# Taking the sixteen Q/K column tiles in the order of their numbers, in a fused attention and quantized-FFN layer on eight cores

## What is computed

```python
xn = layernorm(x)
q, k, v = split(xn @ w_in.T)                  # 16 heads of 64
# windows of 512 tokens; a query sees its own window up to itself
# and the 512 keys before itself (its own and the preceding window)
p = softmax(q @ k.T / 8 + slope[h] * (qi - kj))
attn = (p @ v) @ w_out.T
x_scale = max|xn| per token / 127;  x_q = round(xn / x_scale)
ffn = (x_q @ weight_q.T) * x_scale * weight_scale + bias
out = x + attn + ffn
```

## Time and profile before

| | us |
|---|---|
| median of 2 runs (3992.86 to 4000.87) | 3996.86 |
| the profiled execution, its own time | 3986.59 |
| its span, core 3 (slowest) | 3984.7 |
| spans of the eight cores | 3949.1 to 3984.7 |
| TensorE busy (matmuls) | 2591.0, 65% |
| ScalarE busy | 1769.4, 44% |
| VectorE busy | 1371.6, 34% |
| mean granted TensorE clock | 0.705 of full |

### The profile page before, as it was taken

The page is one execution under the profiler, slowest core; times in us unless marked ns, Lnnn a source line. Parts: engine busy times, 40 slices in busy tenths (PEclk is TensorE's granted clock), DMA queues, the critical chain, the costliest instruction groups (busy, mean ns, idle before and its releaser), DMA issues.

```text
span 3984.7 us, 41683 instructions; the slowest of 8 cores (3949.1 to 3984.7 us)
## 1 busy us (share of the span) xinstructions
PE 2591.0 (65%) x10560; PEld 1031.4 (26%) x10560; DVE 1371.6 (34%) x3552; ACT 1769.4 (44%) x4033; POOL 4.4 (0%) x10
## 2 busy tenths in 40 slices
PE   0466675766766667576676657667576666766777
PEld 0122232222322223222232222223222222322322
DVE  0233342333423244242442423335233333423414
ACT  0252551825616173371733438164281525617355
POOL 0000000000000000000000000000000000000000
PEclk9867668576585857758667675866758677585776
DMA  8101102011020201102011010100101011020100
GB/s 156 62 28 52 36 15 74 5 50 39 13 77 6 85 4 38 50 6 85 4 36 54 32 58 6 61 27 26 63 5 56 34 47 41 11 79 4 42 26 26
DMA packets 79521, 161.00 MB, mean 40 GB/s; under 512 B 8770, under 2 KB 17218, under 8 KB 78914
## 3 DMA queue, kind: packets, MB, share of 16 engines
q1 hardware_dynamic: 76786, 147.85, 10.9%
q0 software_dynamic: 2512, 10.49, 1.6%
HBM read 119.51 MB, written 37.75 MB: 39 GB/s over the span
## 4 chain that ended last, share of the span: by engine, by line
PE 42%; ACT 15%; DMA 14%; DVE 12%; issue 9%; ACTq 5%; DVEq 3%; SPq 0%; POOLq 0%
PE ps L461 14%; ACT pe_buf L652 10%; DMA wqk<-w2bf 9%; PE ps L609 8%; PE ps L702 6%; PE ps L631 6%; PE ps L714 5%; ACTq L105 4%; DMA x_tm<-x 3%; DVEq L105 3%; PE ps L551 2%; ACT zln L533 2%; DVE stt L277 2%; DVE stt L279 1%; DVE pe_buf L665 1%
## 5 line engine op out<-in xcount | busy, mean ns | idle before, releaser
L652 ACT ACTIVATE pe_buf<-ps,ebias_sb 128x128 bf16<-128x128 f32 (+4 forms) x2560 | 912.8, 526 | 190.8 <-PE ps L631 182.6
L461 PE MATMUL ps<-xn_fm,wqk 128*128 128x512 bf16 x2048 | 599.8, 457 | 507.3 <-DMA wqk<-w2bf 506.5
L609 PE MATMUL ps<-pe_buf,v_st 128*65 128x128 bf16 (+3 forms) x2368 | 656.7, 399 | 346.1 <-DVE pe_buf L665 217.2
L665 DVE TENSOR_TENSOR pe_buf<-pe_buf,tripo_sb 128x128 bf16<-128x128 bf16 x1792 | 391.9, 223 | 1086.3 <-ACT pe_buf L652 1041.3
L631 PE MATMUL ps<-q_fm,k_st 64*128 64x512 bf16 (+3 forms) x1792 | 459.8, 434 | 231.5 <-ACT pe_buf L652 223.8
L461 PEld LDWEIGHTS ps<-xn_fm,wqk 128*128 128x128 bf16 x2048 | 220.9, 113 | 884.8 <-issue 751.0
L609 PEld LDWEIGHTS ps<-pe_buf,v_st 128*65 128x65 bf16 x2368 | 271.5, 152 | 675.9 <-issue 604.2
L268 DVE BATCH_NORM_STATS2 stbn<-x_tm 128x6 f32<-128x512 f32 x64 | 43.6, 681 | 1129.1 <-DMA x_tm<-x 1129.1
L472 ACT CAST q_fm<-ps 128x512 bf16<-128x512 f32 x128 | 75.1, 587 | 757.1 <-PE ps L461 757.1
L472 ACT CAST k_st<-ps 128x512 bf16<-128x512 f32 x128 | 75.1, 587 | 639.1 <-PE ps L461 639.1
L702 PE MATMUL ps<-wout_sb,o_fm 128*128 128x512 bf16 x1024 | 259.9, 412 | 0.6 <-DMA o_fm<-o_stage 0.6
(11 more groups left out here) (50 smaller groups left out, 1512.0 us busy)
## 6 DMA issues: line engine op xcount, KB each, us to landing
wqk<-w2bf SPq DMA_DIRECT2D x256, 256.0 KB, 2.7
x_tm<-x SPq DMA_DIRECT2D x16, 2048.0 KB, 7.8
out<-outhf SPq DMA_DIRECT2D x128, 256.0 KB, 2.0
o_fm<-o_stage SPq DMA_DIRECT2D x128, 64.0 KB, 1.9
k_st<-w POOLq DMA_DIRECT2D x2, 2048.0 KB, 17.2
w2bf<-k_st SPq DMA_DIRECT2D x2, 2048.0 KB
wv_sb<-wv POOLq DMA_DIRECT2D x1, 2048.0 KB, 18.1
wout_sb<-wout POOLq DMA_DIRECT2D x1, 2048.0 KB, 18.0
```

Of the source, the lines that this page charges most:

```text
L461: tk = P.op("tensor", lambda e, b=b, ec=ec, fp=fp: e.matmul(out=psum[b][:, :], lhsT=wqk_buf[fp][:, 128 * ec:128 * (ec + 1)], rhs=xn_fm[:, ...
L609: slp=slp, first=pv_first[hh], lastp=lastp: e.matmul(out=psum[ob][0:65, c0:c0 + cw], lhsT=vsl, rhs=pe_buf[:, 512 * slp + (c0 - qsp):512 * ...
L652: sl_pe=sl_pe, ecol=ecol: e.activation(out=pe_buf[:, 512 * sl_pe + a0 - qs:512 * sl_pe + a1 - qs], in_=psum[b][:, a0 - qs:a1 - qs], func=A ...
L665: gm = P.op("vector", lambda e, sl_pe=sl_pe, tloc=tloc, tsel=tsel: e.tensor_tensor(out=pe_buf[:, 512 * sl_pe + tloc:512 * sl_pe + tloc + 128],
```

## The change

It has three edits, two in `emit_qkv` and one in `emit_attn`. The order of the Q/K column tiles becomes 0, 1, ..., 15 in place of 0, 8, 1, 9, ..., 7, 15. The V tiles run with the token chunk in the outer loop and the half in the inner one, in place of the reverse. Each score matmul waits for the latest token of all Q and K tiles and of both halves of V, in place of those of its own pair and half. Nothing is added or removed: the loads, matmuls and copies are the same in number and shape.

```diff
         def emit_qkv(t):
             s_i, n_i, par, slot, pslot, rowbase = tgeom(t)
-            qk_order = [v for pr in range(8) for v in (pr, pr + 8)]
+            qk_order = list(range(16))
...
             v_tok = {}
-            for half in range(2):
-                for tc in range(4):
+            for tc in range(4):
+                for half in range(2):
                     b, bw = banks.acquire()
...
             v_tok = TS[t]["kv"]
+            qk_all = max(qk_tok.values())
+            v_all = max(v_tok.values())
...
-                            waits=bw + [("S", qk_tok[pr2]), ("S", v_tok[pr2 // 4])], inc="T")
+                            waits=bw + [("S", qk_all), ("S", v_all)], inc="T")
```

## The result

| | before | after |
|---|---|---|
| median, us | 4001.9 (10 runs) | 3681.83 (11 runs) |
| profiled execution, us | 3986.59 | 3672.72 |
| its span, us | 3984.7 (core 3) | 3670.8 (core 0) |
| ratio, 95% interval | | 0.9186 (0.916 to 0.9212) |

The change takes 8.1% off; 8.7% was forecast. Between the profiled executions it is 314 us where the prediction had 342. A few executions of each kernel in these runs were disturbed; the ratios leave them out, the medians don't.

A forecast was written before the change was run, and what follows sets the result against it. Waits for wqk loads before the Q/K matmuls (L461) bound the kernel, from neighbouring tiles sharing a buffer. 3986.6 - 342 + 1 = 3646 us profiled, 3655 by the runs' median; forecast 3650 us, 8.7% less, 8 in 10 for 3600 to 3750.

The forecast's parts named there:

- The bound: Q/K projection: 507.3 us idle before L461, waiting for wqk loads, lies on the path that sets the end.
- g: Q/K stage: time from one tile's end to the start of the tile whose load that end releases, 3.01 us.
- The gaps after: Q/K stage after the change: one gap of 1.28 us per two tiles, seven per block, 9.0 us.
- rival (c): Weight loads: overlapping transfers land late, slower than before; with 7.0 us everywhere 88 us slower, 4085 us; chance 0.02.
- The clock: Q/K stage after: low-clock loss of 2.5 us at the start and 1.0 us later, per block.
- Rival (a): Q/K stage: the clock drops as often as before; gain only 242 to 286 us, 3711 to 3755 us; chance 0.17.
- The 5.8 low tiles: Q/K stage before: 5.8 of 16 tiles run at the low clock, from 37.5 us of matmul against 27.7.
- m: Q/K stage: time of one tile of eight matmuls at the full clock, 1.73 us.
- The sum: Q/K stage: 36.7 + 2.5 + 1.0 = 40.2 us against 61.6, 21.4 us less per block, 342 us in all.
- Behind the stage: After Q/K: x load, statistics and exponentials move with the stage; x load issued 4.74 us before its end, as before.
- Rival (b): Dense matmul stretches: the denser stage lowers the clock where it was full; 68 us lost, 3718 us; chance 0.05.
- The score wait: Attention's first score slips about 0.9 us, hidden in 15 blocks by exponentials 11 us later, bare once in the last.

The follow-up runs named there:

- one buffer: The changed kernel with a single weight buffer (`fp = 0`) in place of two: 4572.4 us, ratio 1.1386.
- four buffers: The changed kernel with four weight buffers in place of two, a semaphore for each: 3499.3 us median of four runs, no ratio.
- the old order with alternating buffers: The kernel before, with the weight buffer taken from the tile's position in the order and not its number: 3678.4 us, ratio 0.9156.
- the V order and waits alone: The changed kernel with the old Q/K tile order put back: 4018.6 us, ratio 0.9999.
- the spread normalizations with all waits: Against both early loads, the four normalizations moved behind head pairs 0 to 3, scores waiting for all Q, K and V: 3174.4 us profiled, no ratio.
- both early loads: Four buffers plus first four weight loads issued before the previous output projection and next x load in parts between weight loads: 3246.9 us, ratio 0.806.

## Why the prediction was right, step by step

- **The bound** was read rightly: the time lost before L461 was on the path. Taking 20.3 us out of the stage took 19.6 us out of the block (314/16).
- **g.** Predicted 3.01 us from 143 waits; one buffer measured 3.03 us.
- **The gaps after.** Predicted 1.28 us, seven per block, 9.0 us; measured gaps 1.1 to 1.2 us in the regular stretches and 9.4 us per block with the late landings (8.0 to 9.4 on the eight cores). Staggered loads land no later (2.6 us median against 2.7 in the earlier trace rows), so rival (c) is out. The longest landing grew from 5.5 to 6.8 us, which no term of the sum had.
- **The clock, sized too high.** Predicted 3.5 us per block over full speed (2.5 at the start, 1.0 later). Summing by how much the starts of neighbouring matmuls stand more than 0.216 us apart gives 2.4 us, 1.8 at the start and 0.6 later. Rival (a), as many drops as before, would have left about 600 us of Q/K matmul; there were about 509. The 5.8 low tiles that the prediction counted before are 5.0: 644 of 2048 matmuls took over 0.5 us.
- **The end of a stretch, a term that the sum lacks.** The last matmul of a stretch ends 0.16 us later than its 0.216 us (16 take 3.62 us, not 3.46). The prediction saw this, took it out of m and put it in nowhere, though g counts from that later end. Eight stretches would make 1.3 us per block; late loads split more pairs, and it is 1.8 us.
- **The sum.** In the prediction's terms the stage is 27.7 + 9.4 + 2.4 + 1.8 = 41.3 us, against 27.7 + 9.0 + 3.5 = 40.2; timed directly it is 41.2. That the two miss by only 1 us is in part luck: the clock was too high by 1.1 and the ends of the stretches were missing. Of the 28 us by which the gain fell short, 17 are in the stage and 11 behind it.
- **Behind the stage.** The x load moved with the stage, but not quite by as much. On the slowest cores it landed in 8.8 us in place of 7.9 (means of 15 blocks), and so the first exponential stands 0.7 us farther behind V's last matmul. The landing is no effect of the change: over the eight cores its mean is 8.4 us before and after. What the eight cores do share is the lead: before, the load was issued 5.3 us ahead of the stage's end, since the last tile was often at the low clock (50 of 120), and after it 4.7 (2 of 120). The prediction had 4.74 for both.
- **The Trainium skill on gaps** ("TensorE: Matmul & The Clock Gate", HAM oscillation) describes short bursts of matmuls with transfer waits of 3 to 5 us between them, in which every burst starts at the low clock. One buffer agrees (3.03 us, nine in ten matmuls low). With 3.0 us behind each pair it holds for 5.0 of 16 tiles only, and gaps of 2.0 to 2.5 us, shorter than its case, already brought 12 drops in 26.
- **Rival (b).** In the execution that was timed against the prediction it has fallen: V's group took 222.8 us for 1008 recorded matmuls, 0.221 us each, as in the earlier trace rows, and no core shows another clock than 0.50 and 1.00. The same holds with four buffers, with 24 us of dense matmuls at 1.00 on all eight cores at once. The limiter that the Trainium skill ("TensorE: Matmul & The Clock Gate", part 1) describes, 13/16 of the clock for a whole die once three of its cores run dense matmuls, has rows that fit it elsewhere in this case, though: three other profiled executions show 0.81 on the cores of one die. The prediction's sentence that the rows disagree with it holds for its own trace and no farther. Whether it takes three busy cores to bring it, no run here shows.
- **The score wait.** Predicted 0.9 us slip, hidden. The idle time before the scores for V's eviction (us, times, mean), before and after:

```profile
PE ps L631 <- ACT v_st L493: 5.7, 16, 0.4
```
```profile
PE ps L633 <- ACT v_st L493: 13.2, 16, 0.8
```

The time doesn't notice (0.9999). In the last block, where the slip is bare, the first exponential comes 1.1 us after V's last matmul in place of 0.6. The step was right, with its cover and with its price when the cover is gone.

## What to carry to other kernels

When buffers are chosen by an item's number, look at the order in which the items are taken: two neighbours on one buffer turn double buffering into single buffering with no other sign than a DMA wait in front of every second group. Count cover in tiles: a load of 3.0 us from release to use, against tiles of 1.73 us, needs two tiles ahead and so three buffers. A wait in front of TensorE costs more than its length where it lets the clock fall, and a wider semaphore wait is free only as long as something later holds the same consumer; note what that is, for the next change may remove it.

## What the runs showed of the hardware beyond that

The clock's answer to gaps: 3 us of wait behind every 1.7 us tile kept TensorE at the low level nearly throughout (nine in ten matmuls), the same wait behind every second tile let it rise for 11 of 16 tiles, and gaps of 1.1 to 1.2 us left it at 1.00 once it had risen at the stage's start. x parts of 512 KB put between weight loads of 256 KB on the same queue made those land at 3.8 us median in place of 2.9, with hardly a loss (130.2 us of idle time against 122.9) while three tiles of cover stood ahead.

There is a third clock. Three profiled executions show it on the cores of one die: the old order with alternating buffers (73 to 187 us on each core of die 0), the V order and waits alone (147 to 199 us on die 1), and the spread normalizations with all waits (79, 77, 11 and 4 us on die 1). In the first of them, core 3, a window inside V and V's 64 matmuls, which take 13.98 us at 1.00:

```profile
384.00:400.00 16.00, 16.00 (x62) 6.63 (x61) 11.71 (x17) 4.11 (x7) 0.00 (x0) 0.81 0.22 91
...
385.04 16.98 PE L484 MATMUL ps<-wv_sb,xn_fm 128*128 128x512 bf16 x64
```

The kernel is not what decides it, as far as these traces go: the changed kernel, four buffers and both early loads are as dense or denser and show none of it. When it comes is open.
